# Expert tiles cut into single matrix products and laid evenly through the rounds of a recurrence, with loops on the matrix engine written out

## What is computed

```
s = layernorm-ed recurrence:                                  # 8 sequences of 512 tokens
    xn   = layernorm(x); xn += depthwise_conv3(xn)
    gate = sigmoid(xn @ Wg);  Bm = (xn*sigmoid(xn @ Wi)) @ B.T + b;  Cm = xn @ C.T + c
    step: state = layernorm(state @ A_bar + Bm[t]);  y[t] = Cm[t] * state
    s = (y @ D.T + d) * gate
g = silu(mixture of experts):                                 # 8 experts, 2 chosen per token
    abel = gelu(z @ Wa);  h = gelu(z @ ew1[e] + eb1[e]);  eo = h @ ew2[e] + eb2[e]
    moe  = (sum over the two experts of weight*eo) @ rotations
    k    = sigmoid([abel, moe] @ gc);  ffn = z + abel*(1-k) + moe*k
out = x + s * silu(ffn)
```

## Time and profile before

| what | us |
|---|---|
| median of three runs | 385.67 |
| the profiled execution: its time, its span | 384.9, 383.1 |
| PE busy | 328.0 (86% of the span) |
| DVE busy | 286.5 (75%) |
| ACT busy | 192.8 (50%) |
| POOL busy | 144.3 (38%) |
| mean granted PE clock | 0.954 |

### The profile page before, as it was taken

The page is one execution under the profiler, slowest core; times in us unless marked ns, Lnnn a source line. Parts: engine busy times, 40 slices in busy tenths (PEclk is TensorE's granted clock), DMA queues, the critical chain, the costliest instruction groups (busy, mean ns, idle before and its releaser), DMA issues.

```text
span 383.1 us, 12000 instructions
## 1 busy us (share of the span) xinstructions
PE 328.0 (86%) x4252; PEld 242.1 (63%) x4283; DVE 286.5 (75%) x1381; ACT 192.8 (50%) x545; POOL 144.3 (38%) x186
## 2 busy tenths in 40 slices
PE   1745997989999999989999999889989988879792
PEld 0735884675666666776867878757758734335592
DVE  2989436996777777778877677679999967788844
ACT  1213984410434434655746657748768615444830
POOL 6042000026656664546500006545540047666140
PEclk9995995778999999999999999999999999999997
DMA  7449600003111140785882776875884822122092
GB/s 264 115 111 347 198 3 0 0 4 128 72 41 44 43 135 36 258 297 182 291 272 106 258 251 186 274 235 193 256 246 161 330 67 55 44 50 48 15 144 80
DMA packets 53542, 55.91 MB, mean 146 GB/s; under 512 B 6744, under 2 KB 38655, under 8 KB 53503
## 3 DMA queue, kind: packets, MB, share of 16 engines
q1 hardware_dynamic: 37695, 38.21, 29.7%
q0 software_dynamic: 4960, 10.00, 10.8%
q10 hardware_dynamic: 10848, 7.25, 6.2%
HBM read 14.11 MB, written 18.13 MB: 84 GB/s over the span
## 4 chain that ended last, share of the span: by engine, by line
PE 45%; DVE 36%; issue 7%; DMA 6%; ACT 3%; SPq 2%; DVEq 0%; ACTq 0%
PE bank L1083 9%; DVE wT L974 5%; DMA record<-experts 5%; PE bank L1481 4%; DVE ring L987 4%; PE bank L364 4%; DVE xpad L1239 3%; PE bank L1490 3%; PE bank L1454 2%; PE bank L1447 2%; DVE roots L929 2%; PE bank L1463 2%; DVE Rho L931 2%; PE bank L1378 2%; PE bank L397 2%
## 5 line engine op out<-in xcount | busy, mean ns | idle before, releaser
L1696 POOL DMA_INDIRECT pulls<-expert_rows,slots x64 | 60.6, 948 | 103.4 <-DMA expert_rows<-rows_out 66.5
L1083 PEld LDWEIGHTS bank<-Mrep,wT 32*32 32x32 f32 x2560 | 44.3, 104 | 61.3 <-issue 60.1
L1682 POOL DMA_INDIRECT sorted_rows<-late,slots x64 | 61.7, 965 | 49.1 <-PE bank L1083 40.2
L1083 PE MATMUL bank<-Mrep,wT 32*32 32x64 f32 x2560 | 68.6, 220 | 12.5 <-DVE wT L974 8.6
L1583 ACT ACTIVATE desk<-bank,record 128x128 f32<-128x128 f32 x156 | 48.6, 363 | 33.5 <-PE bank L1481 32.6
L1481 PE MATMUL bank<-desk,record 128*128 128x128 f32 x312 | 55.5, 300 | 4.0 <-DMA record<-experts 4.0
L987 DVE SCALAR_TENSOR_TENSOR ring<-bank,Rho,Dv 128x64 f32<-128x64 f32 x124 | 34.9, 282 | 24.5 <-PE bank L1083 21.6
L1490 PE MATMUL bank<-record,desk 128*128 128x129 f32 x312 | 48.3, 277 | 0.0
L1481 PEld LDWEIGHTS bank<-desk,record 128*128 128x128 f32 x312 | 40.7, 190 | 11.6 <-ACT desk L1577 2.9
L1577 ACT ACTIVATE desk<-bank,cols 128x128 f32<-128x128 f32 x78 | 35.7, 458 | 15.5 <-PE bank L1471 15.5
L364 PE MATMUL bank<-bias,ones 128*128 128x512 bf16 x134 | 39.9, 389 | 3.1 <-issue 2.6
(11 more groups left out here) (329 smaller groups left out, 607.5 us busy)
## 6 DMA issues: line engine op xcount, KB each, us to landing
record<-experts SPq DMA_DIRECT2D x78, 290.5 KB, 3.5
sorted_rows<-zero_rows SPq DMA_DIRECT2D x2, 2496.0 KB, 16.7
expert_rows<-rows_out ACTq DMA_DIRECT2D x12, 322.5 KB
desk<-sorted_rows SPq DMA_DIRECT2D x12, 320.0 KB
X<-in_L_attn_x ACTq DMA_DIRECT2D x4, 512.0 KB, 6.6
out<-X SPq DMA_DIRECT2D x6, 256.0 KB, 3.1
out<-experts POOLq DMA_DIRECT2D x6, 256.0 KB, 5.5
expert_rows<-rows_out ACTq DMA_DIRECT2D x6, 193.5 KB, 4.1
```

Of the source, the lines that this page charges most:

```text
L1083: t = pe.matmul(psY[q], wT[q, 32 * c:32 * c + 32], Mrep[q, c, :], start=(c == 0), stop=(c == 1))
L1682: pool.indirect_dma_start(sorted_rows[h], bass.IndirectOffsetOnAxis(ap=slots[:, j, q:q + 1], axis=0), z_rows[:, q, :], None)\
L1696: pool.indirect_dma_start(pulls[:, n % 3, j, s, :], None, expert_rows[n // (NB // HALVES)], bass.IndirectOffsetOnAxis(ap=slots[:, j, q:q + ...
```

## The change

PE's loop of rounds 1 to 3 is written out. The six matrix products of a tile become single pieces, and `pieces_at` lays the 486 pieces of 81 tile slots (78 and three of lead) over 99 places: 34 places per round (32 steps, one ahead of the boundary, one behind it), less three at the end. A place gets four or five pieces. ACT's answers follow the same table. Consecutive tiles alternate banks without a break at bodies.

The eight C products leave the bodies and round 4's first two steps; each is cut in two and put into steps 0 to 15 of round 4, with one filler product instead of three. The secant's product (L1518) runs once instead of six times. Filler products in rounds 1 to 3 are gone, except near the last boundary.

At a boundary the product by two segments goes to bank 7 with a signal of its own (`second_shift`); it comes second after rounds 0 and 1, first after rounds 2 and 3, and is left out after round 4. The wait for `abel_rows` moves ahead of the boundary of round 0. Mixing of sequences 0 to 3 and their gathers start two turns later. In the tail, the output products of sequence 2 move into step 31 of round 4, those of 3 behind the boundary, those of 4 and 5 ahead of the sums, and the check behind the sums; DVE's and ACT's lists are reordered to fit.

```diff
-        psN, psN2, psK = banks[0][:, S:2 * S], banks[0][:, 2 * S:3 * S], banks[1][:, 0:S]
+        psN, psN2, psK = banks[0][:, S:2 * S], banks[7][:, 0:S], banks[0][:, 5 * S:6 * S]
...
         def tensor_boundary(pe, turn):
             pe.wait_ge(sem("state_T"), turn)
-            pe.matmul(psN, shift[:, :], ends[:, :], start=True, stop=True)
-            pe.matmul(psN2, shift2[:, :], ends[:, :], start=True, stop=True).then_inc(sem("product"), 1)
+            if turn <= 2 * PER:
+                pe.matmul(psN, shift[:, :], ends[:, :], start=True, stop=True).then_inc(sem("product"), 1)
+                pe.matmul(psN2, shift2[:, :], ends[:, :], start=True, stop=True).then_inc(sem("second_shift"), 1)
+            elif turn < ROUNDS * PER:
+                pe.matmul(psN2, shift2[:, :], ends[:, :], start=True, stop=True).then_inc(sem("second_shift"), 1)
+                pe.matmul(psN, shift[:, :], ends[:, :], start=True, stop=True).then_inc(sem("product"), 1)
+            else:
+                pe.matmul(psN, shift[:, :], ends[:, :], start=True, stop=True).then_inc(sem("product"), 1)
...
+        PIECES = 6
+        LEAD = 2
+        ROOM = L + 2
+        EXPERT_ROOM = 3 * ROOM - 3
+
+        def pieces_at(r, place):
+            total, at = PIECES * (TILES + LEAD + 1), (r - 1) * ROOM + place
+            return range(min(total, at * total // EXPERT_ROOM), min(total, (at + 1) * total // EXPERT_ROOM))
...
-            return (98 if n < NB // HALVES else 4 * L + 14) + 8 * (n % (NB // HALVES))
+            return (100 if n < NB // HALVES else 4 * L + 14) + 8 * (n % (NB // HALVES))
-        GATHERS = 82
+        GATHERS = 84
...
         def tensor_tail(pe):
             state_transposes(pe, 0, 3)
+            ssm_products(pe, 0, 4)
+            ssm_products(pe, 0, 5)
+            weighted_sum(pe, 6)
+            pe.wait_ge(sem("state_affine"), 3)
+            weighted_sum(pe, 7)
             pe.wait_ge(sem("close_col"), 1)
             pe.transpose(psF, close[:, 0:1], ident[:, :]).then_inc(sem("close_row"), 1)
-            for n in range(2, NB):
-                if n == 4:
-                    weighted_sum(pe, 6)
-                elif n == 6:
-                    pe.wait_ge(sem("state_affine"), 3)
-                    weighted_sum(pe, 7)
-                ssm_products(pe, 0, n)
+            ssm_products(pe, 0, 6)
+            ssm_products(pe, 0, 7)
...
+                def expert_pieces(r, place):
+                    for piece in pieces_at(r, place):
+                        tile, part = piece // PIECES - LEAD, piece % PIECES
+                        if part < 2:
+                            if 0 <= tile < TILES:
+                                layer1(tile, part)
+                        elif part == 2:
+                            if tile + LEAD < TILES:
+                                rows_transpose(tile + LEAD)
+                        elif 0 < tile <= TILES:
+                            layer2(tile - 1, part - 3)
...
+                pe.wait_ge(sem("abel_rows"), NB + 1)
                 tensor_boundary(pe, PER)
                 keep_warm(pe, 4, 2)
-
-                pe.wait_ge(sem("abel_rows"), NB + 1)
-                with pe.Fori(0, 3) as r:
-                    with pe.Fori(0, 2) as h:
-                        b = r * 2 + h
-                        tile0 = b * BODY
-                        turn = r * PER + h * BODY_STEPS
-                        for i in range(BODY_STEPS):
-                            tensor_step(pe, turn + (PER + i + 1))
-                            if i == 0:
-                                pe.matmul(psK, shift[:, :], start_now, start=True, stop=True)
-                            if 2 <= i < BODY + 2:
-                                layer1(b, tile0, i - 2)
-                            if i < BODY:
-                                rows_transpose(b, tile0, i)
-                            if i >= 3:
-                                layer2(b, tile0, i - 3)
-                            if i == 1:
-                                C_proj(2, b)
-                            keep_warm(pe, FILL_BODY.get(i, 0))
-                    keep_warm(pe, 1)
-                    tensor_boundary(pe, r * PER + 2 * PER)
-                    keep_warm(pe, 4)
+                for r in range(1, ROUNDS - 1):
+                    for k in range(L):
+                        if r == 3 and k == 0:
+                            pe.wait_ge(sem("state_T"), r * PER + 1)
+                            pe.matmul(psK, shift[:, :], start_now, start=True, stop=True)
+                        tensor_step(pe, r * PER + k + 1)
+                        expert_pieces(r, k)
+                    expert_pieces(r, L)
+                    if r == ROUNDS - 2:
+                        keep_warm(pe, 2, 2)
+                    tensor_boundary(pe, (r + 1) * PER)
+                    expert_pieces(r, L + 1)
...
                 for k in range(L):
-                    tensor_step(pe, 4 * PER + k + 1)
-                    if k in (0, 1):
-                        C_proj(k + 5, k + 6)
+                    tensor_step(pe, (ROUNDS - 1) * PER + k + 1)
...
+                    if k < 2 * NB:
+                        C_proj(k // 2, k % 2)
...
+                    elif k == L - 1:
+                        ssm_products(pe, 0, 2)
                     else:
-                        keep_warm(pe, 3, 2)
+                        keep_warm(pe, 1 if k < 2 * NB else 3, 2)
                 tensor_boundary(pe, 5 * PER)
-                keep_warm(pe, 2, 2)
+                ssm_products(pe, 0, 3)
                 tensor_tail(pe)
```

More of the change, by code:

```diff
@@ L1474, in layer1 @@
+                def layer1(tile, k):
+                    b, u = divmod(tile, BODY)
                     at = RECORD_PLACE[u]
                     w, _, _, _ = fields(record[:, at])
[L1476 to L1481 removed]
@@ L1482, in layer1 @@
-                    t.then_inc(sem("pre_hidden"), 1)
-                def layer2(b, tile0, u):
-                    _, w, _, bias = fields(record[:, RECORD_PLACE[u]])
-                    pe.wait_ge(sem("hidden"), tile0 + (u + 1))
-                    pe.wait_ge(sem("rows_copied_out"), tile0 + (u + 1 + BODY - SINCE[u]))
-                    o = out_bank(u)
-                    for k in range(K):
-                        pe.matmul(o, hidden[:, u % 2, k, :], w[k], start=(k == 0), stop=False)
-                    pe.matmul(o, ones_all3[:, :], bias, start=False, stop=True).then_inc(sem("rows_done"), 1)
+                    if k == 0:
+                        pe.wait_ge(sem(f"record{at}"), b * (16 * RECORD_USES[at]) + 16 * (1 + RECORD_TURN[u]))
+                        pe.wait_ge(sem("rows_T"), tile + 1)
@@ L1666, in _ @@
                     mix_piece(dve, n, 13)
+                    if n == 6:
+                        vector_verdict(dve)
                     dve.wait_ge(sem("mixed"), n + 1)
```

129 lines of the change are left out of this document (74 added, 55 removed).

## The result

The changed kernel takes 384.01 us, median of 18 runs (380.14 to 387.98); the kernel before took 388.04 beside it, median of 18 (384.11 to 391.76). The ratio is 0.9897, with a 95% interval of 0.9868 to 0.9926: faster by 1.0%, 4.0 us. Forecast were 378 against 385.67, 2.0%. The sign was right and the time lies in the stated range, but the change brought half of what was forecast. Executions of one kernel lie some 2% apart; ratios and intervals leave out those that lie over 1.5% above the fastest.

The account below looks back on a forecast made before the run. PE was taken to bound round 2 and the tail, DVE round 3, with round 1 near balance. From 384.9 us, terms of -14.0 and +7.0 for fetching the program gave 378; the range was 369.5 to 388.

Parts of the forecast that it names:

- the even load: Rounds 1 to 3: PE's pieces spread at 4.91 products a place; -3.0, -7.0 and -1.5 us by round.
- What bounds the kernel: Rounds 1 to 3 and tail: PE bounds round 2 and the tail, DVE round 3, round 1 near balance.
- Tail, -2.8: Tail: check's wait off PE's path, fillers and a shift gone, an output product moved into round 4; -2.8 us.
- End of round 0, +0.15: Boundary after round 0: shift waits for ACT's copy, +0.3, less 0.15 for a shorter first wait; +0.15 us.
- Round 1, -3.0: Round 1: DVE holds steps at 1.55 us, so 51.6 against 54.6; -3.0 us.
- Round 2, -7.0: Round 2: 30 steps at 1.39 us, so 46.8 against 53.7; -7.0 us.
- Round 3, -1.5: Round 3: two mixing pairs move to round 4, -1.0; secant's first steps and boundary give 0.5; -1.5 us.
- Round 4, -1.3: Round 4's first two steps: half a C product and one filler each, under DVE's 1.26 to 1.4; -1.3 us.
- Records, +1.5: PE's waits for records in rounds 1 and 2, put back after falling out of the sums; +1.5 us.
- fetching the program, +7.0: Written-out rounds 1 to 3: 16 new instruction blocks stop PE at 0.44 us each; +7.0 us.
- The mark that the prediction set: Changed profile: "issue" stops inside sixteen products totalling 0, 7 or 17 us decide between the cases.
- the rival of hidden fetches: Written-out list: all instruction blocks come in time and cost nothing; 371 us, chance 0.25.

Follow-up runs that it names:

- e9: The kernel before with the new order of the tail alone; 385.34 us, ratio 0.9917.
- e3: The changed kernel with the records in six places by turns; 379.44 us, ratio 0.9807.
- the repaired kernel: The changed kernel with fillers where PE idles, six record places by turns and first mixing four turns later; 373.84 us, ratio 0.9643 in its second run.
- e4: The changed kernel with fillers in round 1's first three places and round 3's last two steps, and records in six places by turns; 377.86 us, ratio 0.9753.
- e8_again: Second run of e4 with the mixing of sequences 0 to 3 four turns later; 373.84 us, ratio 0.9643.
- e2: The changed kernel with fillers in round 1's first three places and round 3's last two steps; 377.48 us, ratio 0.9769.
- e5: The kernel before with PE's loops of rounds 1 to 3 written out and records in six places by turns; 386.04 us, ratio 0.9937.
- e6: The kernel before with only PE's inner loop written out, a body of a whole round running three times; 395.95 us, ratio 1.0211.
- e7: e4 with whole tiles laid over the 99 places instead of single products; 380.77 us, ratio 0.9755.
- e8_late_mix: First run of e4 with the mixing of sequences 0 to 3 four turns later; 375.22 us, ratio 0.9684.
- e1: The kernel before with PE's loop of rounds 1 to 3 written out and nothing else; 393.1 us, ratio 1.0181.
- The repair alone: The changed kernel with only its records put in six places by turns (e3); 379.44 us, ratio 0.9807.

## Where the prediction was right and where it failed

The step that failed is the price of rounds 1 to 3. They were put at -11.5 us for the even load, +1.5 for records and +7.0 for stops at fetches, -3.0 in all. The changed kernel has -1.5, but with no such stop. In place of the 8.5 us set against the gain stand five costs, 9.5 us together: 3.5 for late records (1.5 were allowed), 2.1 for tiles cut by a step's product, 1.7 for the half clock in round 1, 1.0 for late gathered rows, and 1.2 in round 3 that is only in part explained. The last four stood at nothing. That 8.5 and 9.5 lie so near is luck. The profiled execution is 4.5 us over the forecast's 378: 1.5 from these rounds, 1.4 from round 4, where the forecast gain didn't come, and 1.6 from a later start of round 0, which the change doesn't touch. Part by part:

*What bounds the kernel.* Right. With nothing late, round 1 runs at DVE's 1.55 a step and round 2 at PE's rate.

*Tail, -2.8.* Right: -2.9 in the changed kernel, -2.7 in e9.

*End of round 0, +0.15.* The later shift costs what was said, the boundary took 3.96 instead of 3.64; the 0.15 for the shorter first wait didn't show.

*Round 1, -3.0.* The floor was right, 51.8 in e3 against 51.6. The changed kernel got 0.6 of it. The prediction said that the clock stays up "since PE has products 1.39 us of every 1.39 to 1.69": that speaks of a mean place, and the first places of round 1 hold one transpose each. The fillers there were removed at no cost in the sum, and the half clock took 1.7. A late record took 0.55.

*Round 2, -7.0.* The changed kernel got 1.7. Three terms were missing. A step was put at 4.91 products of 1.25/6 plus 0.36, which is 1.39; it is 1.46, because sixteen small products between the parts of a tile cost something where they cut it: 0.15 in layer 1's pair, 0.20 in layer 2's (0.32 and 0.33 by starts instead of 0.45 in all). Over 30 steps that is 2.1, and the repaired kernel's 49.5 against 46.8 is mostly this. The gathered rows cost 1.0 at step 30 (2.58 against some 1.5). Late records are nearly all of the rest, with waits of 1.9.

*Round 3, -1.5.* It became +0.75 instead. One late record took 1.07. DVE's busy time fell by 0.8, as the moved pieces say, but its idle time rose by 1.5. The first step takes 1.42 against 1.14: the secant's product now stands ahead of the step's, which starts 0.37 us after it in the trace. The rest is open; no run tried it. Without late records the round took 55.9 (e3) and 55.6 (e4), not the forecast 54.6. The 54.2 of e8_again has four turns of mixing less in it and confirms nothing.

*Round 4, -1.3.* Right in the repaired kernel (45.3 to 44.1), though later mixing was added there; e2, without it, has 43.5. In the changed one the slow clock (its first two steps took 3.2 us against 2.5 in e8_again) and a third "issue" stop took it back.

*Records, +1.5, and fetching the program, +7.0.* Here was the mistake in the mechanism. They were two terms and are largely one. In rounds 1 to 3 the blocks hardly ever stop PE themselves (no stop in the changed kernel, one of 0.59 to 2.31 us each in e5, e6, e7 and e8_late_mix); they go with longer waits for records (4.0 to 8.8 in e1, 7.0 us in time), and no such wait is left once every record has five tiles of lead instead of three at the least. In the changed kernel the waits were 4.4 in all and lengthened the rounds by some 3.5. The repair alone brought rounds 1 and 2 from 106.0 to 102.6, of which 1.7 is the clock that stayed up in that execution; by the ratios it is worth 0.9%, in intervals that overlap. The mark that the prediction set, "issue" stops of 0, 7 or 17 us, read 0 in rounds 1 to 3, which belongs to the rival of hidden fetches. That rival had the stops right and the time wrong (371), since the other costs were missing. The repaired kernel's ratio, 0.9643, makes 371.9 of the 385.67 before, where that rival stood, but with later mixing that no forecast had in it.

What stays open: why a block's arrival stops PE in round 4 and hardly in rounds 1 to 3, and when a given pause brings the clock down.

## What to carry to other kernels

When an edit removes filler work, look at the emptiest place of the new order and not at the mean one; here the clock fell in the first steps of the pipeline. Before a loop is written out or tightened, count how many tiles ahead each transfer may start, and look at the shortest lead: going from three tiles to five there made 7 us of loss vanish, with as many instructions as before. And take the small parts by themselves, since here a reordered tail gave most of what the whole change gave.

## What the runs showed of the hardware

- Writing out a list that had run as a loop made a kernel 7.0 us slower: 32 packets of instructions instead of 15, and PE's waits for records 8.8 us instead of 4.0. All ten waits for a record of over 1 us in the traces end 2.6 to 4.5 us after a packet's start.
- PE's "issue" stops inside a step's products (those of over 0.4 us, the longest 2.31) end 2.2 to 2.9 us after a packet's start, but for one at 3.5. Most packets bring none: the changed kernel has 19 in rounds 1 to 3 and no such stop of over 0.2 us.
- A body of 16 steps took 3 packets in its first round and none in the two rounds after. One of 32 steps took 6 in its first pass, none in the second and 9 around the third, and the branch into that pass cost 5.39 us of PE.
- The granted clock fell to 0.50 for 6.8 us after three pauses of 0.46, 0.86 and 0.48 us within 4 us; in another execution with the same pauses it stayed at 1.00. With nine fillers in those places and four ahead of the last boundary the mean clock of an execution was 0.945 to 0.955; without them it was 0.920 to 0.942, and 0.922 to 0.951 in e3.
- A pair of 128x128 products cut by sixteen 32x32 ones takes 0.69 us by starts instead of 0.54.
